# A two-layer block on one core: a lead of six inner tiles, and a new instruction order on three engines

## The reference, cut to what matters

```python
x = x + ln(attn(ln(x)))
x = x + ln(ffn(ln(x)))

# attn: q, k, v = split(x @ W_qkv.T); 16 heads of 32
q, k = elu(q) + 1, elu(k) + 1
out = q * cumsum(k * v) / (q * cumsum(k) + 1e-9)     # along the sequence
return out @ W_out.T * 32 ** -0.5

# ffn: ternary_quant per group of 64 weights: scale = mean|w|, q = clip(round(w / scale), -1, 1)
gate, up = split(x @ ternary(w_gate_up).T)           # 512 -> 2 * 2048
h = rms_norm(silu(gate) * up)
return h @ ternary(w_proj).T                         # 2048 -> 512
```

## Time and profile before

| what | value |
|---|---|
| median of 3 executions | 1218.29 us (1218.20 to 1219.13) |
| profiled execution, its own time | 1217.17 us |
| its span in the trace | 1215.1 us |
| PE, DVE, POOL, ACT busy | 1110.6, 791.3, 528.3, 441.0 us |
| mean granted clock of PE | 0.963 of full speed |

### The profile page before, as it was taken

The page is one execution under the profiler, slowest core; times in us unless marked ns, Lnnn a source line. Parts: engine busy times, 40 slices in busy tenths (PEclk is TensorE's granted clock), DMA queues, the critical chain, the costliest instruction groups (busy, mean ns, idle before and its releaser), DMA issues. The chain is left out here.

```text
span 1215.1 us, 14590 instructions
## 1 busy us (share of the span) xinstructions
PE 1110.6 (91%) x5376; PEld 661.0 (54%) x5376; DVE 791.3 (65%) x1224; ACT 441.0 (36%) x752; POOL 528.3 (43%) x493
## 2 busy tenths in 40 slices
PE   6995187989989999999999999999999999899997
PEld 5774154544536676445854486446844585454443
DVE  5997757999845848843886268744885278525423
ACT  4232225656522212442234323441344313433432
POOL 1545447788643415441542434342544253215322
PEclk9997587999989999999999999999999999999999
DMA  7021013211003020000210020000200020100000
GB/s 268 1 70 35 24 63 122 87 53 45 1 0 105 1 70 36 1 1 1 70 35 1 1 70 35 1 1 9 93 3 1 1 70 1 35 1 1 35 1 35
DMA packets 29079, 44.97 MB, mean 37 GB/s; under 512 B 1361, under 2 KB 9553, under 8 KB 29009
## 3 DMA queue, kind: packets, MB, share of 16 engines
q1 hardware_dynamic: 29008, 44.05, 11.1%
HBM read 34.60 MB, written 9.44 MB: 36 GB/s over the span
## 5 line engine op out<-in xcount | busy, mean ns | idle before, releaser
L523 PE MATMUL bank<-x3t,wgu_t 128*128 128x512 f16 x1536 | 354.8, 384 | 11.3 <-ACT ht L941 7.6
L1176 POOL TENSOR_TENSOR acc<-acc,ht 128x512 f32<-128x512 f32 x105 | 136.9, 1304 | 276.0 <-ACT ht L975 275.9
L523 PEld LDWEIGHTS bank<-x3t,wgu_t 128*128 128x128 bf16 x1536 | 149.4, 99 | 195.4 <-issue 13.3
L559 PE MATMUL bank<-wproj_t,hid 128*128 128x512 bf16 x896 | 210.3, 380 | 0.0
L1448 DVE TENSOR_TENSOR ht<-ht,bank 128x512 f32<-128x512 f32 x112 | 76.1, 680 | 162.8 <-PE bank L523 128.2
L504 PE MATMUL bank<-xnt,wqkv_hi 128*128 128x512 f32 x672 | 168.7, 393 | 5.8 <-issue 2.7
L1454 DVE TENSOR_TENSOR hid<-ht,hid 128x512 f16<-128x512 f32 x112 | 98.2, 877 | 71.7 <-ACT hid L965 71.6
L559 PEld LDWEIGHTS bank<-wproj_t,hid 128*128 128x128 f16 x896 | 87.7, 98 | 103.5 <-issue 1.5
L504 PEld LDWEIGHTS bank<-xnt,wqkv_hi 128*128 128x128 f32 x672 | 125.7, 189 | 33.0 <-issue 5.7
L965 ACT ACTIVATE hid<-ht 128x512 f16<-128x512 f32 x112 | 70.5, 630 | 186.9 <-DVE ht L1448 175.0
L1118 POOL TENSOR_TENSOR tk<-tq,ts 128x512 f32<-128x512 f32 x28 | 56.4, 2015 | 140.6 <-DVE ts L1376 140.6
(11 more groups left out here) (161 smaller groups left out, 1532.6 us busy)
## 6 DMA issues: line engine op xcount, KB each, us to landing
raw_q<-in_L_ffn_w_gate_up_dram SPq DMA_DIRECT2D x32, 256.0 KB, 2.8
xn<-in_L_attn_x_dram SPq DMA_DIRECT2D x7, 1024.0 KB, 5.1
out_dram<-xn SPq DMA_DIRECT2D x7, 1024.0 KB, 8.6
x<-in_L_attn_x_dram SPq DMA_DIRECT2D x6, 1024.0 KB, 6.6
raw_q<-in_L_ffn_w_proj_dram SPq DMA_DIRECT2D x16, 256.0 KB, 3.0
raw_a<-in_L_attn_W_qkv_dram SPq DMA_DIRECT2D x4, 768.0 KB, 8.4
xn<-in_L_attn_x_dram SPq DMA_DIRECT2D x4, 256.0 KB, 3.5
raw_out<-in_L_attn_W_out_dram SPq DMA_DIRECT2D x1, 1024.0 KB, 12.5
```

What stands on the lines that cost most here:

```text
L523: last = pe.matmul(bank[:], wgu_t[:, k, first_row:first_row + P], x[:, part, k], start=(n == 0), stop=(n == 2 * KD - 1))
L559: last = pe.matmul(bank[:], hid_of(f, part, k)[:, t * P:(t + 1) * P], wproj_t[:, k], start=(k == 0 and part == 0), stop=(k == MT - 1 and p ...
L1176: pool.tensor_tensor(acc[:], acc[:], ht_of(f)[:, m % 2], ALU.add).then_inc(q["acc_done"], 1)
```

## The change

`BEHIND` becomes 6: chunk 0 leads chunk 1 by six inner tiles. The first three hidden tiles of chunk 0 get places of their own (`hid_early`, in what was outt), and so does its sum of squares (`acc_early`). On PE, the units of m = 0 to 5 of chunk 0 and batches 2 to 8 stand ahead of `transpose_x1(1)`, three projections behind it; batch 0 is transposed ahead of `transpose_x1(0)`, batch 1 within the units of m = 0; the projection of attention 1 stands after m = 2 instead of m = 0. The helpers of ACT, POOL and DVE are cut into single instructions, and `start()` of each lists them one by one in a new order. SP issues the halves of the weights in other stretches between its other transfers. The count of the arithmetic operations is the same, and from `attention_of_third` on PE's order is the same. The core of the diff (the lists are cut; `clip` and `round_off` are the two halves of `ternary`, and `den_`, `num_` those of `numden`):

Sizes and places:

```diff
     AHEAD = 3
-    BEHIND = 4
+    BEHIND = 6
+    EARLY = 3
...
         x1_b = sb("x1_b", [P, NT, D], F32, at_sets + 4 * NT * D)
         hid_b = [sb(f"hid_b{m}", [P, 2, N], FP16, (at_sets if m < MT // 2 else at_outt) + 4 * N * (m % (MT // 2))) for m in range(MT)]
+        hid_early = [sb(f"hid_early{m}", [P, 2, N], FP16, at_outt + 4 * N * m) for m in range(EARLY)]
+        acc_early = sb("acc_early", [P, N], F32, at_outt + 4 * N * EARLY)
...
         def hid_of(f, part, m):
 
+            if f == 0 and m < EARLY:
+                return hid_early[m][:, part]
             return hid_b[m][:, part] if f == 1 else hid[:, part, m % HR]
...
         def acc_of(f):
 
-            return acc_b if f == 1 else acc
+            return {0: acc_early, 1: acc_b}.get(f, acc)
```

SyncE:

```diff
-            load_halves(0, RAW)
+            load_halves(0, 3)
             sp.wait_ge(t1_done, KD)
             sp.dma_start(xn[:], x_ch[1]).then_inc(x_loaded, 16)
             sp.dma_start(x1[:], x_ch[0]).then_inc(xres_loaded, 16)
-            load_halves(RAW, 15)
+            load_halves(3, 22)
             sp.wait_ge(att_hi, 2 * KD)
             sp.wait_ge(att_lo, 2 * KD)
             sp.dma_start(x1_b[:], x_ch[1]).then_inc(xres_loaded, 16)
-            load_halves(15, 22)
+            load_halves(22, 30)
             sp.wait_ge(x1_ready, 2 * NT)
             sp.dma_start(out_ch[1], x1_b[:]).then_inc(kept_x1, 16)
-            load_halves(22, 26)
+            load_halves(30, 34)
             sp.wait_ge(t3_done, 2 * KD)
             sp.dma_start(xn[:], x_ch[2]).then_inc(x_loaded, 16)
-            load_halves(26, 2 * NBATCH)
+            load_halves(34, 48)
```

TensorE (`transpose_half`, `unit` and `start`):

```diff
-                if b == 0 and i == 0:
-                    pe.wait_ge(x3t_hi, KD)
-                    pe.wait_ge(x3t_lo, KD)
-                else:
-                    pe.wait_ge(q_out, 2 * b + i)
-                if kind == "gu" and i == 1:
...
+                    if b == 0 and i == 0:
+                        pe.wait_ge(ln2_x, NT)
+                    elif b == 1 and i == 0:
+                        pe.wait_ge(x3t_hi, KD)
+                        pe.wait_ge(x3t_lo, KD)
+                    else:
+                        pe.wait_ge(q_out, 2 * b + i)
...
-                if m == 0 and which == 0:
+                if m == 0:
                     pe.wait_ge(x3t_hi, KD * (f + 1))
...
-                attention_of_first()
-                attention_of_second()
-                feed_forward_of_both()
-                attention_of_third()
...
+                transpose_x_at(1, 0, 1, 2, 3), group_at(0, 8, 9, 10, 11), group_at(1, 0, 1, 2, 3, 4, 5, 6), project_att_at(0, 0, 1, 2, 3)
+                group_at(1, 7, 8, 9, 10, 11), transpose_half(0, 0, 1), transpose_x1_at(0, 0, 1, 2, 3), gate_unit(0, 0)
+                transpose_half(1, 0), up_unit(0, 0), transpose_half(1, 1), transpose_half(2, 0, 1), gate_unit(0, 1)
+                transpose_half(3, 0), up_unit(0, 1), transpose_half(3, 1), gate_unit(0, 2), transpose_half(4, 0), up_unit(0, 2)
+                transpose_half(4, 1), project_att_at(1, 0, 1, 2, 3), gate_unit(0, 3), transpose_half(5, 0), up_unit(0, 3)
+                transpose_half(5, 1), gate_unit(0, 4), transpose_half(6, 0), up_unit(0, 4), transpose_half(6, 1)
+                transpose_half(7, 0, 1), gate_unit(0, 5), transpose_half(8, 0), up_unit(0, 5), transpose_half(8, 1)
+                transpose_x1_at(1, 0, 1, 2, 3), project_first(0, 1, 2), gate_unit(0, 6), transpose_half(9, 0), up_unit(0, 6)
+                transpose_half(9, 1), gate_unit(1, 0), transpose_half(10, 0), up_unit(1, 0), transpose_half(10, 1), project_first(3)
...
```

ScalarE (`hidden_gate`, `hidden_hi`, `hidden_square` and `start`):

```diff
                 elif m == 2:
                     act.wait_ge(q["sq_done"], at(MT, c, 0))
+                    if f < 2:
+                        act.wait_ge(q["h_lo"], 1)
...
                     if m == MT // 2:
-                        act.wait_ge(out_done, NT)
+                        act.wait_ge(FF_MAIN["pr_done"], EARLY)
+                    if m == MT // 2 + EARLY:
+                        act.wait_ge(ss_done, 1)
...
                     if f == 0 and m == 0:
+                        act.wait_ge(out_done, NT)
+                    if f == 0 and m == EARLY:
                         act.wait_ge(out_done, 2 * NT)
...
-                    if m >= HR:
+                    if m >= (HR + EARLY if f == 0 else HR):
                         act.wait_ge(q["pr_done"], at(MT, c, m - HR))
...
-                act.wait_ge(q["h_lo"], at(MT, c, m))
+                if f < 2 and m == 0:
+                    act.wait_ge(q["h_done"], 1)
+                else:
+                    act.wait_ge(q["h_lo"], at(MT, c, m))
...
-                out_hi(0, 0), features(0, 2, True), out_hi(0, 1), features(0, 3, True)
-                cast(0), cast(1), out_hi(0, 2), features(1, 0, True)
-                cast(2), out_hi(0, 3), features(1, 1, True)
-                cast(3), out_hi(1, 0), features(1, 2, True)
-                cast(4), out_hi(1, 1), features(1, 3, True)
-                cast(5), turn(0), turn(1), out_hi(1, 2), x3_hi(0)
-                put_half(0, 0), put_half(0, 1), turn_and_cast(0), out_hi(1, 3)
-                put_half(1, 0), put_half(1, 1), turn_and_cast(1)
-                for m in range(BEHIND):
-                    b = TURNED[m][0]
-                    hidden_gate(1, m), put_half(b, 0), hidden_hi(1, m), put_half(b, 1)
-                    turn_and_cast(b), hidden_square(1, m)
-                x3_hi(1, first_bank=4, x=x3t_b)
...
+                feature_relu(1, 0, 1), feature_exp(1, 0, 1), cast_half(2, 0, 1), out_hi(0, 3), feature_relu(1, 1, 0)
+                feature_exp(1, 1, 0), feature_relu(1, 1, 1), feature_exp(1, 1, 1), cast_half(3, 0, 1), out_hi(1, 0)
+                feature_relu(1, 2, 0), feature_exp(1, 2, 0), feature_relu(1, 2, 1), feature_exp(1, 2, 1), cast_half(4, 0, 1)
+                out_hi(1, 1), turn(0, 1), put_half(0, 0), feature_relu(1, 3, 0), feature_exp(1, 3, 0), cast_half(5, 0, 1)
+                put_half(0, 1), feature_relu(1, 3, 1), feature_exp(1, 3, 1), x3_hi_of(0, 0, 1, 2, 3), cast_half(6, 0, 1)
+                put_half(1, 0), hidden_gate(1, 0), put_half(1, 1), turn(2, 3), cast_half(7, 0, 1), put_half(2, 0, 1)
+                cast_half(8, 0, 1), out_hi(1, 2), hidden_gate(1, 1), put_half(3, 0), out_hi(1, 3), hidden_hi(1, 0)
+                hidden_square(1, 0), hidden_hi(1, 1), put_half(3, 1), cast_half(9, 0, 1), put_half(4, 0), hidden_gate(1, 2)
+                hidden_hi(1, 2), hidden_square(1, 1), put_half(4, 1), cast_half(10, 0, 1), hidden_square(1, 2), turn(4, 5)
...
```

GpSimd (`start`):

```diff
-                norm_x(0), numden(0, 0), norm_x(1), numden(0, 1), numden(0, 2), numden(0, 3)
-                numden(1, 0), divide(0), numden(1, 1), rstd("2", 0), finish_x1_rows(0)
-                divide(1), row_power(0), scale_back(0), norm_x1(1), numden(1, 2), divide(2), scale_back(1)
-                numden(1, 3), divide(3), row_power(1), scale_back(2), divide(4), scale_back(3), divide(5)
...
+                den_guard(0, 3), num_product(0, 3), den_product(1, 0), den_guard(1, 0), num_product(1, 0), divide(0)
+                den_product(1, 1), scale_back(0), den_guard(1, 1), rstd_power("2", 0), num_product(1, 1), divide(1)
+                rstd_bias("2", 0), finish_x1_tile(0, 0, 1, 2, 3), divide(2), rstd_power("3", 0), rstd_bias("3", 0)
+                norm_x1_tile(0, 0), scale_back(1), power_lead(0), power_rest(0), power_take(0), norm_x1_tile(0, 1, 2, 3), divide(3)
+                power_lead(1), power_rest(1), power_take(1), den_product(1, 2), den_guard(1, 2), divide(4), den_product(1, 3)
+                den_guard(1, 3), num_product(1, 2), scale_back(2), num_product(1, 3), scale_back(3), divide(5), scale_back(4)
+                divide(6), power_lead(2), power_rest(2), scale_back(5), divide(7, 8), power_take(2), scale_back(6), divide(9)
+                scale_back(7), power_lead(3), power_rest(3), rstd_power("2", 1), add_square(0, 1), rstd_bias("2", 1)
+                add_square(0, 2), power_take(3), scale_back(8), finish_x1_tile(1, 0, 1, 2, 3), divide(10), rstd_power("3", 1)
...
```

VectorE (`start`):

```diff
-                front(0, 0, False, True), stats_x(1)
-                tile(0, 0), split_x(1), tile(0, 1), tile(0, 2), tile(0, 3)
-                scale(0), tile(1, 0), scale(1)
-                stats_att(0)
-                back_reciprocal(1, 1), front_features(1, 2), front_products(1, 2, True), ternary(0)
-                back_output(1, 1), front_sums(1, 2, True)
-                add_ln2(0), back_lo(1, 1), row_shrink(0)
-                stats_x1(0)
-                scale(2), tile(1, 2), ternary(1), diff(0), scale(3)
-                back_reciprocal(1, 3), x3_lo(0), back_output(1, 3), row_shrink(1), ternary(2), back_lo(1, 3)
-                diff(1), scale(4), ternary(3), diff(2), scale(5)
-                for m in range(BEHIND):
-                    b = TURNED[m][0]
-                    hidden_value(0, m), diff(b + 1), hidden_lo(0, m), ternary(b + 2)
-                    if m == 0:
```

(36 more changed lines are left out.)

833 lines of the change are left out of this document (455 added, 378 removed).

## The result

| | median, us | range | profiled execution | its span | granted clock |
|---|---|---|---|---|---|
| before | 1218.24 | 1216.69 to 1219.13 | 1217.17 | 1215.1 | 0.963 |
| after | 1162.19 | 1161.81 to 1162.78 | 1162.01 | 1160.1 | 0.984 |

The changed kernel takes 0.9542 of the time before (95% interval 0.9525 to 0.9558): 56 us less, where 26 were forecast. The sign was right, the size was less than half, and 1162 lies outside the range of 1182 to 1206. PE's busy time fell from 1110.6 to 1095.4 us, since less of it runs at the lower clock, DVE's from 791.3 to 773.0, and POOL's rose from 528.3 to 542.2.

A forecast was written before the change was run, and what follows sets the result against it. No engine bounds TensorE's two holes (49.9 us idle) but a chain made long by the order of each engine's work; 3 + 12 + 13 + 4 - 6 = 26 us gained gives a median of 1192, range 1182 to 1206.

The forecast's parts named there:

- Attention of chunk 0: Step 1, chunk 0's attention: an earlier `back_lo` shortens TensorE's three waits for features; 3 us gained, bounds 0 and 4.4.
- Projection to x3t: Step 2, from chunk 0's attention projection: earlier residual, norm and split make x3t whole at 129.9 instead of 142.1; 12 us.
- To the projection of chunk 1: Step 3, x3t to chunk 1's attention projection: six leading units, batch 0 already turned; projection ends at 158.3, lead 28 us.
- Input of chunk 1: Step 4, up to chunk 1's input: six units and eight halves cover its norm chain; lead on paper 32 us.
- Clashes: Step 5, by step 4: `diff` and `hidden_lo` run longer beside POOL, 9.4 us; 6 taken off, bounds 0 and 9.4.
- Plateau and tail: Step 6, from there to 365.8: same work either way; 0 for the plateau, 4 either way; 0 for the tail, -2 to +3.
- the clashes: Rival: chunk 1's `diff`, `hidden_lo` and `back_lo` up to step 4 run near their longest; gain about 13 us, 1205; chance 0.14.
- the head-of-line wait: Rival: an engine early at a list entry holds all behind it; two waits of 8 us, 1208; chance 0.1.
- the slower case: Rival: with both chunks, VectorE's list makes each tile's round longer than TensorE's 10 us; 1222 at 3 us per tile; chance 0.06.
- no change: Rival: nothing happens, since TensorE's waits only move; 1218; chance 0.03.
- the walk holds with nothing taken off: Rival: the walk without the deduction for clashes, and the hole's end brings a little more; 1185; chance 0.07.
- three signs of being wrong: Gate before 130 but chunk 2's group after 350; `diff` median over 1.9 us; VectorE gap over 5 us between 127 and 180.

The follow-up runs named there:

- lead_hand: Changed kernel with lead of six, early places and TensorE's order kept, but the other three engines' lists written by the old loops: 1223.45 us, ratio 1.0051.
- plateau_before: Kernel before plus eight statistics instructions on VectorE, 5.1 us in all, results unused, in units 8 to 11 of chunk 0: 1217.0 us, ratio 0.9993.
- late_norm: Changed kernel with GpSimd normalising the third chunk late again, behind the squares of unit 15 and two more; VectorE's list left: 1170.79 us.
- tail_first: Kernel before with GpSimd's norm of the third chunk and VectorE's cuts of its turned tiles moved earlier in the tail: 1212.01 us, ratio 0.9954.
- hand_from_176: Changed kernel up to 176 us of its trace, then ScalarE, GpSimd and VectorE in the hand order of the kernel before: 1187.64 us.
- value_first: Kernel before with chunk 1's hidden value ahead of a weight batch's sums and maxima in VectorE's plateau: 1222.5 us, ratio 1.0038.

## Why the prediction was wrong in size

The sum was 3 + 12 + 13 + 4 - 6 + 0 = 26 us. Measured at the same points it is 4.5 + 12.5 + 14.6 + 3.6 + 0 + 19.6 = 54.8.

1. *Attention of chunk 0*: 3 said, 4.5 measured; the bound was 4.4. Right: TensorE's three waits are gone.
2. *Projection to x3t*: 12 said, 12.5 measured (17.0 less 4.5). The wait for x3t is one piece of 11.59 us, as foretold. Two runs put the new lists' worth up to x3t at 14.6 and 20.5 us, beside 15 on paper.
3. *To the projection of chunk 1*: 13 said, 14.6 measured. That the number fits is in part luck. The step counted on the two more leading units and on batch 0 turned in the hole; with these and the lists by hand the stage is 4.4 us shorter (lead_hand), and the other 10 come only with the new lists. What they do there can be read: they keep the halves ready that the units take (from the first gate unit to this projection TensorE waits for a difference three times, 8.4 us, in lead_hand and never in the changed kernel). The step also left out that ScalarE's first hidden tile of before waited until the projection of chunk 1 was done, which left VectorE idle for most of the 13.1 us that the prediction read in the earlier trace rows and did not explain. Before, on ScalarE and VectorE:

```profile
169.46 0.63 ACT L965 ACTIVATE hid<-ht 128x512 f16<-128x512 f32 x1 [11.72 <-issue]
170.13 0.69 DVE L1454 TENSOR_TENSOR hid<-ht,hid 128x512 f16<-128x512 f32 x1 [11.05 <-ACT hid L965]
```

No run tried the early places alone, so their share of the 4.4 us is open.

4. *Input of chunk 1*: 4 said, 3.6 measured.
5. *Clashes*: -6 said, nothing to take off measured: the leads by step 4 hold all clashes and are still above the walk. The mean of `diff` fell from 1513 to 929 ns and that of chunk 1's low parts from 1300 to 1124; the clip and the rounding grew. VectorE's groups in the changed kernel:

```profile
L1393 DVE TENSOR_TENSOR yq<-yq,wb 128x1024 bf16<-128x1024 bf16 x24 | 22.3, 929 | 1.7 <-POOL yq L1111 1.7
L1597 DVE TENSOR_TENSOR hid_b<-ht_b,hid_b 128x512 f16<-128x512 f32 x16 | 17.9, 1124 | 4.4 <-ACT hid_b L972 4.3
L1386 DVE TENSOR_SCALAR yq<-yq 128x1024 bf16<-128x1024 bf16 x24 | 16.4, 691 | 0.2
L1379 DVE TENSOR_SCALAR yq<-yq 128x1024 bf16<-128x1024 bf16 x24 | 13.6, 579 | 0.9 <-POOL yq L1104 0.9
```

The differences took 36.3 us before and 22.3 after; clip and rounding 22.0 and 30.0. Together 58.3 and 52.3. For the 24 differences POOL's rest at their start was 23.1 us before and 9.6 after, and less this they took 13 us in either kernel. A length that holds a wait for POOL is no length of work: it shrinks when other work comes first, as plateau_before shows. Adding up clashes as if each were work was the error. The Trainium skill, "SBUF — State Buffer", section "Who interferes with whom", says that VectorE and GpSimd hold one shared port in turns; these lengths agree in kind.

6. *Plateau and tail*: 0 said, 19.6 measured, 8.9 in the plateau (44.1 - 35.2) and 10.7 in the tail (54.8 - 44.1). This is the step that broke the range. It priced the old tail's loss at 35.6 - 29.4 = 6.2 us from busy time. The work there is 104 matmuls at 0.216 us (a unit of eight takes 1.73 by the starts), four transposes at 0.44 and the column sums at 0.8, 25.1 us; the changed kernel does it in 24.8, from 286.14 to 310.95. The loss was 10.7, and the idle time told little over half of it. Of the rest, 2.9 us are the lower clock, which busy time holds: 4.93 and 3.52 us for blocks that take 3.62 and 1.89 at full clock. Before:

```profile
341.01 4.93 PE L523 MATMUL bank<-x3t_b,wgu_t 128*128 128x512 f16 x16
...
353.98 3.52 PE L523 MATMUL bank<-x3t_b,wgu_t 128*128 128x512 f16 x8
```

The plateau took 118.7 us from 211.5 on and holds 437 such matmuls and 264 short ones at 0.055 (33 halves of eight, 0.44 each), 109 us: a loss of 10, of which 6.4 showed as idle. It takes 109.8 now, for 440 and 240 of them, 108 us. The prediction left both losses where they were, though the change rewrites the lists there too. In the tail the loss is a head-of-line wait (late_norm, tail_first); in the plateau the new lists take it away (hand_from_176), and which waits of the old order it was stays open.

Of the rivals, the clashes, the head-of-line wait, the slower case and no change did not happen, and "the walk holds with nothing taken off" was the nearest, at 1185; it too put nothing for the last step. The mark "the first group of chunk 2 is near 340" failed by 29 us, "the gate near 127" and "the projection ends 158 to 162" by 2 and 3 on the good side. None of the three signs of being wrong came: the group of chunk 2 starts at 311, the median of `diff` is 0.69 us, and VectorE's longest gap between 127 and 180 us is 1.7 us.

## What to carry to other kernels

Where in-order lists hand work round, a longer lead alone can be worth nothing: with a lead of six this kernel took 1223 us with the lists in loops and 1162 with the new ones. Price a new order in every stage it covers, the ones that look nearly full too. Count a stage's work from the number of matmuls at full clock, not from busy time, and take the difference from its length as what can be won. And add a few idle instructions to an engine before you lighten it: 5.1 us of them cost 4.6 in the one kernel and 1.0 in the other, and that tells whether that engine's work counts there.

## What the runs showed of the hardware

- A short stall costs more than its idle time: in late_norm TensorE, which had waited 1.0 us in the 110 us before, waited 3.4 us in four pieces, the longest 2.35. The next 16 matmuls took 6.26 us, not 3.62, most of them at a granted clock of 0.50.
- A difference of 128x1024 bf16 on VectorE takes 0.55 to 0.6 us and whatever POOL's instruction of the moment has left (17 of them in three runs: 29.7, 26.5 and 20.5 us with 20.3, 17.0 and 10.5 left on POOL). So VectorE at 93% busy took 5.1 us more work for nothing.
- The same clash can be moved: in value_first chunk 1's low parts went from 1518 to 2232 ns on average and the differences from 1747 to 1206, without a change in what either computes.
